# TensorE's idle-time filler in a four-layer kernel: transposes of the identity instead of products of it, and eleven new places for it

## What is computed

```python
x = x + _L0_xattn_ref(_layernorm(x), ctx, ...)       # a scan over 64 context rows, mean, projection
x = x + _L0_ffn_ref(_layernorm(x), ...)              # 32 experts, best 6, at most 96 tokens each, and a shared one
x = x + _L1_xattn_ref(_layernorm(x), ctx, ids, ...)  # 16 heads, compressed keys, rotary, masked softmax
x = x + _L1_ffn_ref(_layernorm(x), ...)              # 8 experts, best 2, rows weighed by their score, a shared one
x = x + _L2_xattn_ref(_layernorm(x), ctx, ...)       # fp8-rounded inputs, 8 groups, own and cross attention
x = x + _L2_ffn_ref(_layernorm(x), ...)              # ternary weights, hidden width 704
x = x + _L3_xattn_ref(_layernorm(x), ctx, ...)       # 16 heads of 16
x = x + _L3_ffn_ref(_layernorm(x), ...)              # 16 experts, best 2, two shared ones
```

## Time and profile before

| | us |
|---|---|
| median of 3 runs | 1157.14 |
| lowest and highest run | 1154.38, 1159.71 |
| profiled execution, its own time | 1154.36 |
| its span, first to last instruction | 1153.1 |
| PE busy | 1012.9 (88%) |
| DVE busy | 759.1 (66%) |
| ACT busy | 633.6 (55%) |
| POOL busy | 526.4 (46%) |
| mean granted clock of TensorE | 0.936 |

### The profile page before, as it was taken

The page is one execution under the profiler, slowest core; times in us unless marked ns, Lnnn a source line. Parts: engine busy times, 40 slices in busy tenths (PEclk is TensorE's granted clock), DMA queues, the critical chain, the costliest instruction groups (busy, mean ns, idle before and its releaser), DMA issues.

```text
span 1153.1 us, 18626 instructions
## 1 busy us (share of the span) xinstructions
PE 1012.9 (88%) x6092; PEld 815.4 (71%) x6092; DVE 759.1 (66%) x2019; ACT 633.6 (55%) x1824; POOL 526.4 (46%) x582
## 2 busy tenths in 40 slices
PE   4967998177997888899999999999999999898897
PEld 2453655045585678888988888889898878677685
DVE  3766322265666447878888888787877589777444
ACT  1431443002024354689797878888888745563253
POOL 1441677343654363244545454544443236353453
PEclk8877999588997898999999999999999999997999
DMA  9130698920003765010101020101000025005674
GB/s 392 44 124 17 184 220 210 246 65 1 1 1 142 231 217 189 1 56 7 60 1 61 1 61 1 61 2 60 1 24 1 1 97 156 1 2 187 207 283 160
DMA packets 57264, 108.89 MB, mean 94 GB/s; under 512 B 13840, under 2 KB 35216, under 8 KB 55248
## 3 DMA queue, kind: packets, MB, share of 16 engines
q1 hardware_dynamic: 47920, 89.71, 23.7%
q0 software_dynamic: 9248, 18.00, 6.1%
HBM read 79.19 MB, written 27.42 MB: 92 GB/s over the span
## 4 chain that ended last, share of the span: by engine, by line
PE 53%; DVE 20%; issue 7%; POOL 7%; DMA 6%; ACT 6%; SPq 1%; DVEq 0%; POOLq 0%; ACTq 0%
PE bank L200 25%; PE bank L209 8%; PE bank L2475 3%; DVE a_qn L2665 3%; DMA sum<-f_ys,f_index 3%; PE bank L1264 2%; PE bank L217 2%; PE bank L1787 2%; POOL a_qk_rstd L260 2%; PE bank L2462 2%; ACT a_p L2900 2%; POOL f_xs L2105 2%; PE bank L499 1%; POOL a_q_rstd L260 1%; ACT a_p L2893 1%
## 5 line engine op out<-in xcount | busy, mean ns | idle before, releaser
L3014 POOL TENSOR_TENSOR a_p<-a_p,a_tot 128x128 f32<-128x128 f32 x64 | 51.0, 816 | 203.3 <-DVE a_tot L2636 203.3
L200 PE MATMUL bank<-a_w_high,a_in 128*128 128x128 f32 (+1 forms) x512 | 122.4, 282 | 3.8 <-ACT a_p L2893 1.6
L200 PE MATMUL bank<-a_w_low,a_in 128*128 128x128 f32 (+1 forms) x512 | 118.6, 279 | 0.0
L200 PEld LDWEIGHTS bank<-a_w_high,a_in 128*128 128x128 f32 x512 | 97.7, 191 | 5.9 <-ACT a_kx L2869 2.1
L200 PEld LDWEIGHTS bank<-a_w_low,a_in 128*128 128x128 f32 x512 | 97.8, 191 | 0.0
L2687 DVE TENSOR_REDUCE a_top<-bank 128x2 f32<-128x512 f32 (+1 forms) x96 | 56.8, 601 | 30.5 <-PE bank L2475 18.0
L2849 ACT ACTIVATE a_qn<-bank,a_q_shift,a_q_rstd 128x128 f32<-128x128 f32 x128 | 48.3, 461 | 40.7 <-POOL a_q_shift L263 40.7
L2665 DVE TENSOR_SCALAR a_qn<-bank,a_qk_minus,a_qk_rstd 128x128 f32<-128x128 f32 x192 | 64.0, 402 | 5.5 <-POOL a_qk_rstd L260 2.8
L200 PE MATMUL bank<-a_proj_high,a_catq 128*128 128x256 f32 x256 | 63.9, 288 | 1.0 <-issue 1.0
L2475 PE MATMUL bank<-a_kt,a_qt 128*128 128x256 f32 x256 | 62.3, 386 | 0.0
L2922 ACT ACTIVATE a_cat<-bank,l_ismooth 128x256 bf16<-128x256 f32 x128 | 50.4, 483 | 21.3 <-PE bank L2515 21.3
(11 more groups left out here) (427 smaller groups left out, 3065.6 us busy)
## 6 DMA issues: line engine op xcount, KB each, us to landing
experts<-in_experts SPq DMA_DIRECT2D x49, 384.0 KB, 4.4
f_expert<-in_experts SPq DMA_DIRECT2D x31, 384.0 KB, 5.9
third_shelf<-in_groups SPq DMA_DIRECT2D x8, 1024.0 KB, 6.9
f_got<-f_xs SPq DMA_DIRECT2D x10, 516.0 KB, 8.8
third_shelf<-in_groups SPq DMA_DIRECT2D x8, 512.0 KB, 4.2
f_got<-f_ys SPq DMA_DIRECT2D x8, 512.0 KB, 5.2
f_xs<-blank_zero SPq DMA_DIRECT2D x1, 3999.0 KB, 21.5
l_expert<-in_experts SPq DMA_DIRECT2D x10, 384.0 KB, 7.7
```

Of the source, the lines that this page charges most:

```text
L200: ins = pe.matmul(out, lhs, rhs, start=start and n == 0, stop=stop and n == len(pairs) - 1, skip_group_check=shared)
L3014: g_.tensor_tensor(cross_probs(m, ti), cross_probs(m, ti), over(m.tot[n % 2][:, first:first + HPG], SC), ALU.mult).then_inc(*s["cross_weig ...
```

## The change

`pass_time` makes n transposes of the identity in place of n products of it. All counts of its existing calls stay. Eleven calls in the text are new: 64 and 18 in layer 0's feed-forward part, 28 and 40 in layer 1's attention, 30 (layer 1) or 10 (layer 3) ahead of the second half's turn in the feed-forward parts, 12 ahead of the first shared result in layer 1, 6 in each `ranks` and 10 and 14 in the shared steps of layer 3, and 6, 5 and 8 in layer 3's attention. No wait is added but one for `score_copied`, and none is taken away. The waits for x in layer 1's attention are written out ahead of the filler; they were the first ones of `turn_rows_tensor` before.

```diff
 def pass_time(k, bank, n):
-    ident = k.c["ident"]
-    for _ in range(n):
-        k.pe.matmul(bank[:, 0:P], ident, ident, start=True, stop=True)
+    if n:
+        turns(k, [(bank[:, 0:P], k.c["ident"])] * n)
...
     on.wait_ge(*s["facts_set"].at(1))
+    pass_time(k, k.bank[4], 64)
     on.wait_ge(*s["mask_ready"].at(1))
...
     on.wait_ge(*k.kq_scaled.at(H1 // 2))
+    pass_time(k, k.bank[PICK_BANKS[0]], 18)
     for r in range(NT):
         on.wait_ge(*s["pick_ready"].at(r + 1))
...
-    turn_rows_tensor(k, s, k.rows, rows_of(s), [r for x in k.x_ready for r in x])
+    for x in k.x_ready:
+        for r in x:
+            on.wait_ge(*r)
+    pass_time(k, k.bank[0], 28)
+    turn_rows_tensor(k, s, k.rows, rows_of(s))
...
             on.wait_ge(*s["turn_ready"].at(1))
+            if i == 0:
+                pass_time(k, k.bank[6], 40)
             soft_flip_tensor(k, s, m.soft, i, (6, 7), s["divided"].at(i + 1))
...
         on.wait_ge(*s["facts_set"].at(3 if p.weighed_rows else 4))
+        if not p.weighed_rows:
+            pass_time(k, bank[2 if half else 5], 6)
         on.wait_ge(*s4["mask_ready"].at(half + 1))
...
     for r in k.x_ready:
         on.wait_ge(*r[0])
+    pass_time(k, bank[2], 30 if p.weighed_rows else 10)
     turn_half_tensor(k, s4, 1, m.rows, rows_of(s4))
...
+            if not p.weighed_rows and r in (3, 4):
+                pass_time(k, bank[3], 10 if r == 3 else 14)
...
+                if p.weighed_rows and n == 0:
+                    pass_time(k, bank[3], 12)
                 on.wait_ge(*s["swi_turned"].at(p.step(n) + 1))
...
+        if r == NT + 3:
+            on.wait_ge(*s["score_copied"].at(2 * NT))
+            pass_time(k, bank[0], 6)
+        if r == NT + 5:
+            pass_time(k, bank[2], 5)
...
+        if r == 3:
+            pass_time(k, bank[2], 8)
         if 0 <= r - 3 < NT:
             soft_flip_tensor(k, s, soft, r - 3, (2, 3), s["powered"].at(r - 2))
```

## The result

| | before | after |
|---|---|---|
| median, us | 1156.0 (5 runs, 1151.32 to 1159.71) | 1145.18 (5 runs, 1143.54 to 1147.02) |
| ratio, 95% interval | | 0.9914, 0.9889 to 0.994 |
| profiled execution, us | 1154.36 | 1146.68 |
| its span | 1153.1 | 1144.6 |
| mean granted clock | 0.936 | 0.96 |

The change makes the kernel 10.8 us faster by the medians, 9.9 by the ratio and 8.5 us by the spans of the two profiled executions; the forecast was 8.5 us. The experiments ran on several chips of the same type, and on some of them the kernel before takes 1170 to 1172 instead of 1155 to 1156 us. A ratio always compares with the kernel before on the same chip, and so it is the ratio, not the time, that is set beside another experiment's. It is not simply the quotient of the two medians printed, which can differ from it by up to 0.3%.

A forecast was written before the change was run, and what follows sets the result against it. Bound: idle TensorE then working at half clock, plus layer 2's fillers on the path; elsewhere its own work at full clock. Terms 0.6 + 2.2 + 1.7 + 1.7 + 2.7 + 1.0 - 0.65 - 0.8 = 8.5 us, giving 1148.6 us, range 1142 to 1156.5.

The forecast's parts named there:

- One filler's price: Everywhere: a transpose takes 0.109 us at full clock and 0.23 at half; a product 0.22 and 0.43.
- the third rival: Transposes hold the clock less than products: layers 0 and 1 gain nothing, layer 2's head runs low; 1162 us, chance 0.09.
- Transposes hold the clock: On TensorE: a transpose works for the clock at least nearly as a product of equal length; all new places' gains need it.
- (a): Layer 0, 64 fillers ahead of the mask and 18 ahead of the picks: 0.6 us gained, between 1.3 lost and 2.0 gained.
- (b) to (d): Layer 1: 2.2 us gained by 28 in attention, 1.7 by 40 in the softmax, 1.7 by 30 in the feed-forward part.
- (d): Layer 1's feed-forward part, 30 fillers: 1.7 us gained, not 2.5, since POOL's ninth scatter is the next bound.
- the second rival: Fillers end too early, the clock falls in the remaining gaps, layers 0 and 1 gain nothing: 1154.9 us, chance 0.12.
- (e): Head of layer 2, existing fillers shortened: first projection ends at 459.1 instead of 461.8, 2.7 us gained (0 to 4.3).
- (h): Layer 2's head, 449 to 460 us: halved fillers leave gaps, one more clock fall likely, 0.8 us lost (0 to 3).
- Long stretches at 0.50 in layer 2: Layer 2: their appearance in the clock was named as one sign that the prediction is wrong.
- (f): The last unit's 12 fillers, 2.94 us on the path before: 1.0 us gained (0 to 1.5).
- (g): Layer 3, six fillers at round `NT + 3` behind the last flip, where TensorE has no gap: 0.65 us lost.

## Why the prediction was right, point by point

- **One filler's price** was right. 64 transposes take 7.21 us at full clock (0.11 each), 28 take 5.62 in a stretch mostly at half (0.20), and the six 0.65. In the sum of the third rival 117 transposes should stand in place of 113, which moves it by 1 us.
- **Transposes hold the clock**, and bring it back: 228 to 236.3 us above, and the experiment with products. The Trainium skill's contrary rule ("TensorE: Matmul & The Clock Gate", Part 4, PE-mode transpose) is not what these rows show; the third rival, whose extreme it is, fell.
- **(a) Layer 0** was the term of the sum that was mis-sized: 0.6 us taken, 2.2 measured at the picks, 2.1 more at the shared expert, 5.0 by the time x is complete (+2.63 to -2.32). The clock was feared to be lost again in the 3.4 us between the filler's end and the mask; in this execution it was not, and the first pick waited for 1.26 us with TensorE ready. And the picks were taken as the end of the effect, while the low stretch at 107.8 to 114.6 us behind them is gone here too. How much of this is the fillers' and how much is luck the other traces say. Of nine traces with these fillers six have the fall at 84 to 91 us that the prediction feared, with the 18 fillers at 3.0 to 4.2 us, and four have a low stretch at 105 to 113 us; the three without the fall are the three in which everything came 2.5 us later from the start. On the chips without stops the part from the start of the table to x complete brings 5.0, 3.4 and -0.2 us in the three traces that there are, and the kernel before, in its trace with the pauses, loses some 3 us there against itself. The 2.2 us at the picks return in the third of these (58.24 and 102.28 against 58.07 and 104.31); what stands behind them does not. The run without layer 0's calls gave 1.9 us with an uncertainty of 3.
- **(b) to (d) Layer 1**: 2.2, 1.7 and 1.7 forecast, 2.0, 1.7 and 1.7 measured (-2.32, -4.32, -6.05, -7.73). The 16 transposes took 1.94 us where 1.9 was forecast. The bound by POOL was the right one: TensorE's own work is further ahead than 1.7 us (the second half's slots come 9.0 us sooner, 361.65 against 370.61), and the ninth scatter follows the eighth at 0.31 us. The sign that the clock should read 1.00 behind 357 us came true in part: it did for the transposes and the logits and fell to 0.51 at 355.6 to 362.5 us under the shared expert, as the second rival had it for the gap that is left. Here it costs nothing, since POOL is next.
- **(e) and (h) Layer 2's head**: 2.7 gained and 0.8 lost forecast, 3.1 gained (-7.73 to -10.84) and 2.5 lost (-10.84 to -8.35) measured. The head behaved as worked out: the first turn starts 4.4 us sooner after x (447.71 and 435.51 us, less 7.8), the rounding of the inputs 1.2 us sooner, and `a_qk_stats` 2.3 (461.80 and 451.67) where 2.7 was forecast. The loss has its mechanism right and its size wrong. One fall of the clock was counted; there are four stretches, 451.2 to 454.6, 464.9 to 468.3, 478.5 to 485.3 and 495.6 to 502.4 us, 20.4 us in all where the kernel before has 3.4, and the last, in the first flip, is on the path. Long stretches at 0.50 in layer 2 were a sign of being wrong; they are there, but products do no better in their place, and twice the filler takes most of them away (0.97 instead of 0.84): it is the shorter filler, not the transpose.
- **(f)** 1.0 forecast, 0.9 measured. **(g)** 0.65 lost forecast, 0.63 measured (-9.24 to -8.61).

The sum of what was measured, 5.0 + 2.0 + 1.7 + 1.7 + 3.1 - 2.5 + 0.9 - 0.6 = 11.3 us, is near that of the medians, 10.8; against it the forecast missed 4.4 us in (a) and had 1.3 too much in (e) and (h). (b) to (d), (f) and (g) were right in mechanism and size. The equality of 8.5 and 8.5 in the profiled executions is chance: it holds only with the 2.6 us that the second one lost before the first edit, and with a layer 0 that went better than in the other traces. What the prediction lacked altogether is the dependence on the chip: on the one chip with stops on which the changed kernel ran the gain is 0.3%, inside what the prediction calls the same. A part of the reason is shown: (d) takes a gap out of POOL's row of scatters, and with it the time in which TensorE's results got through, so that (d) costs some 3 us there instead of bringing 1.7. The rest, in layer 0, is not worked out.

## What to carry to other kernels

A cheap filler in front of a long wait pays where the work behind it was on the path at half the clock; count for every gap what the filler leaves open, and follow the clock past the wait, to the next stretches, before sizing it. Shortening a filler that already stood in a gap is a change of its own, with a price of its own. And a gain measured on one chip is to be measured on another when indirect DMAs run in a row beside it.

## What the runs showed of the hardware that was not expected

- On two chips, in five traces, ACT got nothing from TensorE for 13 to 14 us and DVE nothing for 8 to 11 while POOL issued indirect DMAs every 1.27 us, and both went on some 2.5 us after the last; on a third one of that kind a pause of 4 us in the row cut ACT's wait to 3.0 us. The stop sets in some 9 us after the first scatter of a row (360.58 to 369.37 us), and after the pause the next scatters did not bring it back before the shared expert had ended. On the first chip the same row of 16 goes by without a stop (the changed kernel's first trace), as does layer 0's row of gathers there and on the chip of the three experiments with pauses. Whether TensorE's work or only its signals are held, and by what, is open: its records show the work done at 372.3 us, but the ends of its records are modelled.
- The clock came back in a row of nothing but transposes of a constant, at 0.50 until 232.6 us and 1.00 from 232.9.
- The same kernel's low stretches lie in part elsewhere in every execution. The changed kernel's two traces share those of the first flip (495.6 us, and 507.8 with the 12.6 us that the second is behind), while only the second has those at 84.3 to 87.7 and 105.0 to 111.8 us. So a single pair of traces can be off by 2 to 4 us in a place where nothing was changed, as at 41 to 45 and at 1041 us.
- The profile's row of the clock can lack a stretch: after, it says 1.00 at 41 to 45 us, where eight products take 3.67 us as they do at 0.50 (1.94 at 1.00). The distance of the records is the check.
